# Reordering TensorE's work inside an attention head: late value groups around a maximum pair, two score tiles together

## The reference, cut to what matters

```
t   = layernorm(x)
qkv = t @ w_qkv + b_qkv                          # 12 heads of 32 channels
a   = softmax(q*scale @ k^T + rel_h + rel_w)     # 1024 x 1024 per head
x   = x + (a @ v) @ w_proj + b_proj
x   = x + moe(layernorm(x))                      # 8 experts, top 2, 40 slots per group and expert
```

## Time and profile before

| | us |
|---|---|
| median of 3 runs | 587.12 (586.67 to 587.63) |
| the profiled execution | 584.53 |
| its span | 582.7 |
| TensorE busy in the span | 565.6 (97%) |
| DVE, ACT, POOL busy | 385.3, 282.2, 192.8 |

### The profile page before, as it was taken

One profiled execution on the slowest core, in us unless ns is written; L12 is line 12 of the kernel. 1 busy time (PEld: TensorE's weight loads), 2 busy tenths in 40 slices (PEclk: granted clock), 3 DMA queues, 4 the chain that ended last, 5 costly groups with the idle time before them and its releaser, 6 DMA issues.

```text
span 582.7 us, 11988 instructions
## 1 busy us (share of the span) xinstructions
PE 565.6 (97%) x4673; PEld 470.1 (81%) x4673; DVE 385.3 (66%) x817; ACT 282.2 (48%) x397; POOL 192.8 (33%) x130
## 2 busy tenths in 40 slices
PE   7999999999999999989989999999999999999996
PEld 7787765555555555549879999999999999999994
DVE  6648886888888888437898855453675554467623
ACT  4454233555555555563555344544555454455424
POOL 2300036888888888898340000000000000000002
PEclk9999999999999999999999999999999999999999
DMA  7256057455555552120605345344524444344203
GB/s 224 88 108 138 10 114 142 100 106 104 107 100 105 98 104 50 42 91 20 204 0 193 134 136 168 114 161 155 163 86 158 163 128 151 129 164 126 79 1 109
DMA packets 42917, 66.61 MB, mean 114 GB/s; under 512 B 5058, under 2 KB 35640, under 8 KB 42742
## 3 DMA queue, kind: packets, MB, share of 16 engines
q1 hardware_dynamic: 42870, 65.98, 41.4%
HBM read 44.42 MB, written 1.57 MB: 79 GB/s over the span
## 4 chain that ended last, share of the span: by engine, by line
PE 83%; POOL 5%; DVE 5%; ACT 4%; issue 2%; DMA 1%; POOLq 0%; SPq 0%; ACTq 0%; DVEq 0%
PE ps L941 22%; PE ps L957 22%; PE ps L708 9%; PE ps L716 9%; PE ps L601 8%; PE ps L689 6%; POOL acc L509 3%; ACT prob L1123 2%; PE ps L968 1%; PE ps L634 1%; DVE tl L1468 1%; DMA xs<-in_x 1%; PE ps L645 1%; POOL dsp L540 1%; PE ps L976 1%
## 5 line engine op out<-in xcount | busy, mean ns | idle before, releaser
L1123 ACT ACTIVATE prob<-ps 128x1024 f32<-128x1024 f32 x96 | 95.5, 1024 | 96.7 <-PE ps L708 95.1
L509 POOL TENSOR_TENSOR acc<-acc,prob 128x1024 f32<-128x1024 f32 x47 | 113.2, 2408 | 5.5 <-POOL acc L509 0.5
L941 PE MATMUL ps<-xeh,wih 128*128 128x320 f32 x288 | 89.6, 311 | 1.0 <-ACT xeh L1180 1.0
L957 PE MATMUL ps<-hh,woh 128*128 128x320 f32 x288 | 89.2, 310 | 0.0
L957 PE MATMUL ps<-hh,wol 128*128 128x320 f32 x288 | 89.0, 309 | 0.0
L941 PE MATMUL ps<-xeh,wil 128*128 128x320 f32 x288 | 89.0, 309 | 0.0
L957 PE MATMUL ps<-hl,woh 128*128 128x320 f32 x288 | 89.0, 309 | 0.0
L941 PE MATMUL ps<-xel,wih 128*128 128x320 f32 x288 | 89.0, 309 | 0.0
L708 PE MATMUL ps<-qm,km 64*128 64x512 f32 x576 | 82.8, 399 | 1.5 <-ACT prob L1123 0.6
L548 POOL CAST dpc<-dpt 120x1024 fp32r<-120x1024 f32 (+1 forms) x3 | 3.1, 1039 | 240.6 <-PE ps L977 216.5
L1357 DVE CUSTOM_DVE_ANT_1 ps<-ps,relhn 128x512 f32<-128x512 f32 x96 | 64.4, 713 | 19.4 <-PE ps L689 18.3
(11 more groups left out here) (172 smaller groups left out, 948.3 us busy)
## 6 DMA issues: line engine op xcount, KB each, us to landing
raw_i<-in_L_ffn_wi SPq DMA_DIRECT2D x32, 576.0 KB, 5.1
raw_o<-in_L_ffn_wo SPq DMA_DIRECT2D x32, 576.0 KB, 4.1
km<-kp SPq DMA_DIRECT2D x24, 256.0 KB, 4.0
qm<-qh SPq DMA_DIRECT2D x24, 192.0 KB, 4.0
xs<-in_x SPq DMA_DIRECT2D x8, 384.0 KB, 4.6
qm<-relw SPq DMA_DIRECT2D x24, 128.0 KB, 4.0
qm<-relh SPq DMA_DIRECT2D x48, 64.0 KB, 2.3
qm<-ql SPq DMA_DIRECT2D x24, 64.0 KB, 2.9
```

Source lines behind the costliest of these rows:

```text
L509: nc.gpsimd.tensor_tensor(acc[:, :], acc[:, :], prob[:, slot_of(j, t), :], ALU.add).then_inc(sum_add, 1)
L941: last = mm(bank(k, SLOTS), w[:, b, c, k * P:(k + 1) * P], xe[:, c, e, :], start=c == 0 and n == 0, stop=c == DC - 1 and n == 2)
L957: last = mm(bank(3 + c, SLOTS), w[:, b, k, c * P:(c + 1) * P], h[:, b, k, :], start=s == 0 and k == 0 and n == 0, stop=s == UNITS - 1 and ...
L1123: run(prob[:, slot_of(j, t), :], ps[:, 2 * (t % 2) * BANK:2 * (t % 2 + 1) * BANK], ACT.Exp).then_inc(exp_done, 1)
```

## The change

In the heads from 1 on, `values(*former, 2)` is moved ahead of the maximum pair 3 of the next head; `values(*former, 3)` stays behind it. At the end of a head, the maximum pair 1 of the head two on is moved from between the score tiles 6 and 7 to behind tile 7. In head 0, pairs 0 and 1 of head 2 are moved from behind `values(h, b, 1)` to ahead of it. No instruction is added or removed, and the lists of the other engines are the same.

```diff
                 scores(h, n, b, 0)
                 if first:
                     pe.wait_ge(v_dve, NT)
+                if not first:
+                    values(*former, 2)
                 next_max(3)
                 if not first:
-                    values(*former, 2)
                     values(*former, 3)
...
                 if not first:
                     after_max(0)
                 scores(h, n, b, 6)
-                if not first:
-                    after_max(1)
                 scores(h, n, b, 7)
-                values(h, b, 1)
                 if first:
                     after_max(0)
-                    after_max(1)
+                after_max(1)
+                values(h, b, 1)
                 after_max(2)
```

## The result

The changed kernel takes 580.28 us (median of 6 runs, 579.37 to 581.79) against 586.56 for the kernel before in the same comparison (585.91 to 587.63). The ratio is 0.9895, with a 95% interval of 0.9879 to 0.991: 5.3 to 7.1 us faster. The profiled execution took 579.37 us with a span of 577.6: 5.2 and 5.1 less than before. So the profiled executions differ by 5.2 and the medians by 6.3; the experiments come back to that difference.

A forecast was written before the change was run, and what follows sets the result against it. TensorE (PE) was taken to bound the kernel, with two bubbles per head. Gains 9 x 0.39 + 10 x 0.05 + 1.08, say 5.1 us, off the median 587.12 gave 582.0; range 579.8 to 585.1, faster 0.87.

The forecast's parts named there:

- the three parts: Gains at the end of heads 1 to 9, start of heads 1 to 10, end of head 0: 3.51 + 0.50 + 1.08 us.
- End of heads 1 to 9: From score tile s6 to value group v1: 1.73 us in place of 2.12, gain 0.39 per head.
- the bubble of p3: In pair M1, the load of maximum block p3 waits for DVE's reduction of p0; claimed to vanish.
- Start of heads 1 to 10: From score tile s0 to s1: 3.59 us in place of 3.64, gain 0.05 per head.
- The pair alone: Maximum pair M3 between value groups v2 and v3: taken as 0.45 us, between 0.23 and 0.65.
- the two meetings: Changes of operand shape on either side of M3, about 0.11 us each, added to the pair's 0.23.
- The rival in which each side costs twice the 0.11: M3 between value groups takes 0.65 us: 2.0 less gain, time 584.0; chance 0.22 together with missed margins.
- End of head 0: M0 right behind s7, v1 covers DVE's chain; s0 of head 1 at 92.56 in place of 93.64, gain 1.08 us.
- The thin margins: At M2 and M4, banks of p2 and p6 free 0.06 us early; rival of failure: 584.5, chance 0.22 with dear pair.
- The sign of a failed margin: Waits of weight loads on `rmax` appearing at M2 or M4 would show the prediction wrong.
- The slower rival: DVE gets p2 and p6 later and becomes the pace: 0.2 us more per head, time 589; chance 0.05.

The follow-up runs named there:

- the second execution: Profiled execution of the changed kernel run again with no edit; 580.37 us against 585.79 for the kernel before, ratio 0.9902.
- The two comparisons at equal clock: Kernel before against the changed kernel run again (4.3 us apart, 5.4 over all runs), and against only head 0's end changed (1.2 apart; median 584.17).

## Why the prediction was right

The forecast was 582.0 (579.8 to 585.1), faster at 0.87; it came to 580.28. The profiled span was forecast at 577.6 and is 577.6, but that exactness is partly luck: the three parts gave 0.6 more than forecast, and the turn of the loop, which the forecast did not have, took 0.7. Of the 1.7 by which the median is below the forecast, 0.6 is the kernel before (586.56 in place of 587.12 in the full comparison), and the rest goes with the clock, below.

- **End of heads 1 to 9: right, a little small.** 0.42 per head for 0.39; the bubble of p3 is gone, and alone this part gave 3.7 us in the runs (9 x 0.42 = 3.8).
- **Start of heads 1 to 10: right.** 0.08 for 0.05. The pair alone takes 0.43 for the estimated 0.45, so the two meetings simply add; alone this part gave about 0.7. The rival in which each side costs twice the 0.11 is not borne out.
- **End of head 0: right.** p3 at 90.80 (forecast 90.79), v1 at 91.22, s0 at 92.56, all as worked out; alone 1.0 in the trace.
- **The thin margins held.** The timeline of DVE shows them:

```profile
153.52 0.76 DVE L1356 CUSTOM_DVE_ANT_1 ps<-ps,relhn,rpart 128x512 f32<-128x512 f32 x1 [0.72 <-PE ps L689]
154.20 0.14 DVE L1356 DVE_READ_ACCUMULATOR2_ANT rmax<- 128x1 f32 x1
...
164.51 0.76 DVE L1356 CUSTOM_DVE_ANT_1 ps<-ps,relhn,rpart 128x512 f32<-128x512 f32 x1 [0.20 <-PE ps L689]
165.19 0.14 DVE L1356 DVE_READ_ACCUMULATOR2_ANT rmax<- 128x1 f32 x1
```

  The reductions of p6 and p2 are read out at 154.34 and 165.33; with the 0.05 of the earlier trace rows PE may go on at 154.39 and 165.38, and M4 and M2 begin at 154.42 and 165.41. 0.03 each, not 0.06, but both loads of each pair go together. The sign of a failed margin that the prediction gave, waits on `rmax` at M2 or M4, was badly chosen: such rows stand there before and after alike. What tells is that M2 and M4 still begin 1.00 behind the value group.
- **Missed: the turn of the loop.** The prediction had every head at 14.63. They are at 14.57, and two at 14.93: minus 0.7 us. The margins explain why: a wait met just in time costs nothing by itself, but a branch behind it has lost its cover. The sum with the measured terms is 9 x 0.42 + 10 x 0.08 + 1.08 - 0.72 = 4.94, the 4.9 of the stretch (the second execution has 4.6).
- **Missed: the clock.** The prediction took the profiled execution of before, which lies 2.6 below its median, and carried the saving over unchanged. That execution had the full clock through the attention, while more than half of the runs had a mean of 0.996 or less. Head 0's sparse end, which the change removes, goes together with such runs: with the old end 19 of 51 runs had 0.997 or more (before 13 of 33, starts only 5 of 12, ends only 1 of 6), with the new end 35 of 44. A mean of 0.993 and less, which takes two such stretches (the trace with both, at 13 to 17 and 95 to 99 us, has 0.993), occurs in 16 of the 51 and in none of the 44. A mean of 0.998 needs none: in both profiled executions of the changed kernel (0.998) the only windows below the full level lie at the very end of the span, from 576 on, where PE has no work left. The two comparisons at equal clock put this at 1.1 to 1.2 us of the difference of the medians; with the 5.1 of the profiled executions that makes the 6.3. That a run lost its clock at this place was seen in one trace; for the others it is inferred from the means. Not every drop is there: in that same execution and in two with the new end (the loop written out, and value group 0 moved) one lies in the first 20 us.
- **The slower rival** (DVE the pace) never came near: DVE waits 0.72 for p6 in the rows above.

## What to carry to other kernels

Measure a pipelined engine from start to start: its busy share of 97% hid two waits of 0.4 us per head, and they vanished by putting 0.7 and 1 us of independent work between a block and the one that needs its buffer. Before filling a bubble, list what else it covers (here a loop's branch, elsewhere a second wait), for that comes next. Where some runs show a lower mean clock, look in the trace of such a run for the place at which the engine only trickles; removing it brought as much again as the wait itself at the end of head 0 here.

## What was not expected of the hardware

- A pair of matmuls of one shape between two groups of another takes 0.43 us: its own 0.23 and 0.2 for both changes, however short the piece between.
- The branch of TensorE's loop costs nothing or 0.33 to 0.42 us, depending on how early the last wait ahead of it is met.
- After three microseconds with 10 matmuls the granted clock was at its lower level for 3.4 us, at a cost of 1.3 us in that execution; in the kernel before, with the same end of head 0 and as few matmuls, it stayed up.
